# A wait for landed rows ahead of every span of sixteen gathers, in a graph layer on one core

## The reference

```python
edge_index = jnp.stack([src, dst])
xn = _layernorm(x, axis=-1)
# _L0_gnn_ref(xn, edge_index, weight, bias):
summed = jax.ops.segment_sum(x[src], dst, num_segments=n)
deg = jax.ops.segment_sum(jnp.ones_like(src, dtype=x.dtype), dst, num_segments=n)
agg = summed / jnp.maximum(deg, 1.0)[:, None]
out = jnp.concatenate([x, agg], axis=-1) @ weight
```

## Time and profile before

| what | value |
|---|---|
| time before, median of 3 runs | 5559.33 us (5557.41 to 5565.59) |
| the profiled execution's own time | 5560.58 us |
| its span | 5558.8 us |
| mean granted TensorE clock | 0.801 |
| GpSimd busy | 2839.8 us, 51% |
| TensorE busy (matmuls) | 3511.5 us, 63% |
| gathers of line 787 | 1664, 1611.5 us busy, idle 902.0 us before them |

### The profile page before, as it was taken

How to read it: one execution, slowest core, us unless ns; L and a number is a source line. 1 busy time by engine, 2 the same in 40 slices (tenths; PEclk the granted TensorE clock), 3 DMA queues, 4 the chain that set the end, 5 groups by cost and what they waited for, 6 DMA issues and landing times. The chain is left out here.

```text
span 5558.8 us, 46231 instructions
## 1 busy us (share of the span) xinstructions
PE 3511.5 (63%) x12937; PEld 2291.2 (41%) x12938; DVE 2083.0 (37%) x4892; ACT 802.4 (14%) x1970; POOL 2839.8 (51%) x2937
## 2 busy tenths in 40 slices
PE   0688888888577767777242766666666666669300
PEld 0455555555455545555121443434343434346200
DVE  5455566565566555444010111112011111103278
ACT  4111111111011111111010101111111111112000
POOL 2666666666666666666657144444445353530420
PEclk6898999899788888888675888788877878789755
DMA  7444444444455555655121111111111111111297
GB/s 254 116 112 111 114 113 113 110 112 111 112 133 148 148 145 149 166 152 151 20 62 19 32 46 35 42 39 43 38 42 46 35 46 36 46 31 63 87 255 257
DMA packets 381413, 540.56 MB, mean 97 GB/s; under 512 B 120315, under 2 KB 297819, under 8 KB 381144
## 3 DMA queue, kind: packets, MB, share of 16 engines
q0 software_dynamic: 119136, 234.44, 19.2%
q1 hardware_dynamic: 243119, 288.12, 16.2%
q10 hardware_dynamic: 19016, 16.48, 0.9%
HBM read 392.03 MB, written 146.74 MB: 97 GB/s over the span
## 5 line engine op out<-in xcount | busy, mean ns | idle before, releaser
L787 POOL DMA_INDIRECT rows<-xn_rows,gsrc x1664 | 1611.5, 968 | 902.0 <-issue 458.8
L1353 POOL DMA_INDIRECT nb<-route_rows,idx x1024 | 1001.5, 978 | 1087.4 <-DVE msg L1428 772.7
L1092 PE MATMUL PS<-rows,oh 128*128 128x257 f32 x3328 | 908.3, 426 | 339.9 <-issue 215.3
L1682 PE MATMUL PS<-arena,hid 128*125 128x256 f32 x3200 | 773.2, 400 | 524.3 <-ACT hid L1643 311.5
L1674 PE MATMUL PS<-x2g,arena 128*128 128x500 f32 x1600 | 759.4, 634 | 314.8 <-issue 154.5
L1682 PEld LDWEIGHTS PS<-arena,hid 128*125 128x125 f32 x3200 | 633.5, 199 | 680.5 <-issue 577.6
L1092 PEld LDWEIGHTS PS<-rows,oh 128*128 128x128 f32 x3328 | 693.4, 214 | 470.9 <-issue 284.3
L1617 DVE TENSOR_TENSOR y_sb<-PS,b_b 125x512 f32<-125x512 f32 x200 | 128.7, 686 | 2010.5 <-PE PS L1682 1466.4
L1674 PEld LDWEIGHTS PS<-x2g,arena 128*128 128x128 f32 x1600 | 321.2, 204 | 732.1 <-issue 540.1
L1643 ACT ACTIVATE hid<-PS,b_sb 128x500 f32<-128x500 f32 x400 | 270.2, 678 | 1551.1 <-PE PS L1674 762.5
L1164 PE MATMUL PS<-own_w,p_t 128*125 128x512 f32 x400 | 228.8, 656 | 77.6 <-ACT s_t L1052 45.4
(11 more groups left out here) (304 smaller groups left out, 3088.6 us busy)
## 6 DMA issues: line engine op xcount, KB each, us to landing
y_rows<-y_sb SPq DMA_DIRECT2D x100, 512.0 KB
arena<-y_rows SPq DMA_DIRECT2D x100, 512.0 KB
rows<-xn_rows,gsrc POOLq DMA_INDIRECT x1664
nb<-route_rows,idx POOLq DMA_INDIRECT x1024
sum_rows<-kept SPq DMA_DIRECT2D x104, 128.5 KB
x_rows<-x SPq DMA_DIRECT2D x100, 128.0 KB
hid<-x_rows SPq DMA_DIRECT2D x100, 128.0 KB
m_in<-sum_rows SPq DMA_DIRECT2D x100, 125.5 KB
```

The source lines that it names most:

```text
L787: pool.indirect_dma_start(out=rows[w][h][:, q, 0:D], out_offset=None, in_=xn_rows, in_offset=bass.IndirectOffsetOnAxis(ap=gsrc[:, s * HU + ...
L1092: last = mm(SUM[:, 0:D + 1], oh[w][h][:, q, :], rows[w][h][:, q, :], start=h == 0 and q == 0, stop=h == 1 and q == HU - 1)
L1353: pool.indirect_dma_start(out=nb[b % NBUF][:, c, :], out_offset=None, in_=route_rows, in_offset=bass.IndirectOffsetOnAxis(ap=idx[:, b * W ...
L1682: last = mm(Y[j % 2][e // 2][0:NP, (e % 2) * D:(e % 2 + 1) * D], hid[:, 4 * e + k, j * NP:(j + 1) * NP], w2_sb[:, e, k, :], start=k == 0, ...
```

## The change

Ahead of the first half of every span but the first, GpSimd also waits for the four semaphores of the other buffer, up to the count that says that all sixteen gathers of the span before have landed. Nothing else is changed, and no other engine's stream.

```diff
                 for s in range(NS):
                     g, h, w = s // 2, s % 2, s // 2 % 2
                     pool.wait_ge(s_used[h], g + 1)
+                    if h == 0 and g:
+                        for of_quad in s_rows[1 - w]:
+                            pool.wait_ge(of_quad, ((g - 1) // 2 + 1) * 16 * QUAD)
                     for q in range(HU):
                         pool.indirect_dma_start(out=rows[w][h][:, q, 0:D], out_offset=None, in_=xn_rows,
                                                 in_offset=bass.IndirectOffsetOnAxis(ap=gsrc[:, s * HU + q:s * HU + q + 1], axis=0)
                                                 ).then_inc(s_rows[w][(h * HU + q) // QUAD], 16)
```

## The result

The changed kernel takes 5590.07 us (median of 6 runs, 5578.1 to 5592.61) beside 5561.88 us for the kernel before (6 runs, 5557.41 to 5567.54). By the medians it is slower by 28 us. The prediction, 5544 with a range up to 5580, was wrong in sign and range; rival 2 named 5590.

The account below looks back on a forecast made before the run. Bound: the coupling by which in-flight gathers hold back TensorE's increments, neither engine's work. Terms 5 + 8 - 13 - 6 - 10 = -16 us on 5560.6 us gave 5544 us; range 5515 to 5580.

Parts of the forecast that it names:

- rival 2: Span starts, second half: landing follows the increment, so the wait starts after the 2.0 us pause; 31 us, 5590; chance 0.25.
- The cover at the 97 starts (cost 0): Span starts where GpSimd already pauses, typically 2.0 us: rows land 1.5 us after the last issue, so cost 0.
- 0.15 us each span if met: Wait instructions on GpSimd at span starts: 0.15 us a span, passing to the end in the second half, +8 us.
- The wait at starts without a break (+5): Six span starts without a pause lose up to 1.2 us each, plus a few slow landings: +5 us, bounds 0 and 15.
- -13: Long gather run at the start: pauses bring ScalarE's first copy near 174 rather than 187.25 us; bounds 0 and -30.
- -6: Span starts at 1450 and 1542 us: a break recovers TensorE's 9.29 us idle and the like; bounds 0 and -12.
- -10: Usual rounds, 280 to 1400 us: starting spans 0.15 us later puts most of 18 on the short side; bounds 0, -27.
- rival 3: Whole block much faster: increments get through at once after every pause, all gains reach their bounds; 5495 us; chance 0.06.

Follow-up runs that it names:

- the kernel with met waits: The change's four waits at 102 span starts, but for rows of the span two back, against the kernel before: 5563.04 us, ratio 1.0003.

## Why the prediction was wrong

**The cover at the 97 starts (cost 0): the step that failed.** I put the landing, 1.5 us after the issue, beside a break of 2.0 us, and took the rest for slack. The landing was right: 1.48 us. But the break of 2.0 us was for one wait on the gather; the new one, a separate instruction, passes 0.41 us after the landing (0.35 of it until the semaphore is raised), and the gather starts 0.72 us behind it: 2.6 us. The 0.6 us that are over are the least cost at a start whose break was 2.0 us. With the longer ones it is 63 us in all, of which the mid-span break gives 47 back. I had priced the waits as instructions (0.15 us each span if met), and met they cost nothing that shows; I hadn't asked what a wait costs that ends late in an instruction of its own. They were not five instructions either, as I had it, but two, with two waits each. And I had no term for TensorE's increments coming later at half of the starts.

**The wait at starts without a break (+5).** There were some, and each took 2.6 us and not 1.5: too small, by about 1 us at six starts.

**The gains (-13, -6, -10).** The earlier increments that I expected did come: the first copy moved from 187.25 to 156.05 us, TensorE has no gap over 1.8 us left between 1457 and 1484 us, and over all spans ScalarE's copy comes 1.4 us after the sums instead of 3.3 (medians). What failed is the step from there to time. An earlier increment shortens the kernel only if its receiver sets the pace, and in the first part, where I booked most of the gains, GpSimd's round of 24.4 us stayed what it was; the gather at 198.52 us is 0.75 us later than before, and the run with the wait in the first part alone gained nothing (1.0010). There the gains were 0; whether the gap at 1450 gave anything can't be told apart from the loss around it.

**The price in the second part.** Rival 2 had the place right (second half, GpSimd's own round), its test (spans over 0.25 us longer, nothing won in the first half) came out at 0.54 us up to 2170 and 0.23 after, 0.42 us in the mean, and its sum, 31 us, is near the 28 measured. Its reason was off: it wasn't that the new wait started after the 2.0 us break, but that it ended later than the old one for being separate. That the sum is near is in part luck: 0.3 us a start and 15 us for slow landings stand for a growth of 52 us at the second part's span starts and 32 us given back in the middle of its spans. Between the starts of spans 52 and 103 GpSimd falls 32 x 0.54 + 19 x 0.23 = 21.6 us behind, nearly all of the 22.7 by which the last gather is late. At the block's end it is 26.6 us, at the kernel's 31.8 in this one pair of executions; the medians say 28.

**The range.** Half way from 5544 to the 5495 of rival 3 is 5520, not 5515. It changes nothing here.

**The rule.** That one should wait late (the Trainium skill, DMA: Bandwidth & Descriptors, "Rules for kernel authors") I had set aside since "the pause is there already". The runs side with the rule, and closely: at the same gather the wait costs 0.35%, one gather later nothing, at twice the places 3.6%.

**What stays open.** That TensorE's increments of `s_used` take effect late can be read from the traces, which record a semaphore's increments too. In the kernel before they stand 3.2 us after the end of the matmul that makes them (median of 203 found), and 166 of the 203 fall in one of GpSimd's breaks; with a quarter of the gathers they stand 0.01 us after it. So the delay goes with the gathers. That landing alone lets them through doesn't fit every start: at 49 starts of the changed kernel they come well after the landing, as at 2404.26, where the break is 3.64 us long. Neither is explained by a run here. Open too is why a break less a span costs 364 us, and how much of it is the earlier demand; and why the gathers land later in the kernel that waits ahead of every half.

## What to carry to other kernels

An idle stretch that ends at one wait doesn't hide a second wait that ends sooner: count from the second one's release through its own instruction to the restart of the engine (here 0.07 + 0.72 us, where a wait on the gather took 0.26), and compare that with the end of the stretch. If an instruction needs two waits, give the one that ends last to the instruction itself, or hang the other on the next instruction; one gather's distance was worth 0.5% here. And book an earlier signal as a gain only where its receiver sets the pace.

## What the runs showed of the hardware

- GpSimd starts a gather at the earliest 0.72 us after a separate wait instruction that had to wait (the least and the median alike, in each of five kernels), and 0.26 us after the release if the wait rides on the gather. A separate wait that is met passes earlier, 12 us before its own gather in the kernel with met waits.
- One separate wait instruction held two of the added waits (206 instructions for 412 waits), a gather one.
- The last packet of a gather of 128 rows of 1 KB ends 1.48 us after the end of its 0.95 us issue, 1.9 to 2.1 us in the kernel that waits ahead of every half, and its semaphore has the last increment 0.35 us after that. The Trainium skill, DMA: Bandwidth & Descriptors, "Anatomy of one DMA — SWDGE (gpsimd) path", gives 2.0 us and the bytes over 436 GB/s, by which an estimate for 128 KB is 2.3 us. The trace has 2.43 us to the last packet and 2.8 us to the semaphore.
- With a quarter of the gathers TensorE's granted clock was 1.00 (2.4 GHz) from 500 to 900 us, where it was 0.92 from 500 to 1000 before, and its sums took 785.7 us busy where they took 908.3.
- A longer run of gathers without a break didn't make a span shorter here: with 16 in place of 8, and the buffer's last reader asked for earlier, a span took 28.1 us and not 24.4 in the first part.
